# Reordering VectorE's list and the turn of the choice in the experts' stage of a four-layer program

## The reference

```
# layer 0, first half: a routed and shared feed-forward with top 2 of 8 experts per token -> x
# layer 0, second half: "expert choice", added to its input
scores = einsum('BTC,CE->BTE', x, gate_w)
probs  = softmax(scores)                        # over the 8 experts
top_p, top_idx = top_k(transpose(probs), cap)   # each expert takes 8 of the 32 tokens of a sequence
xin = take_along_axis(x, top_idx)
h   = gelu(einsum('BElC,ECH->BElH', xin, w1))   # H = 512
y   = einsum('BElH,EHC->BElC', h, w2) * top_p
out = zeros.at[b, top_idx].add(y)
# layers 1 to 3: an LSTM, an RNN and a leaky cell, each with a feed-forward
```

## Time and profile before

| | us |
|---|---|
| median of 3 runs | 560.34 |
| lowest, highest | 558.55, 560.71 |
| the profiled execution, its own time | 560.55 |
| its span in the profile | 559.2 |
| PE busy | 526.6 (94%) |
| DVE busy | 435.0 (78%) |
| ACT busy | 358.9 (64%) |
| POOL busy | 181.8 (33%) |

### The profile page before, as it was taken

How to read it: one execution, slowest core, us unless ns; L and a number is a source line. 1 busy time by engine, 2 the same in 40 slices (tenths; PEclk the granted TensorE clock), 3 DMA queues, 4 the chain that set the end, 5 groups by cost and what they waited for, 6 DMA issues and landing times.

```text
span 559.2 us, 10400 instructions
## 1 busy us (share of the span) xinstructions
PE 526.6 (94%) x3320; PEld 452.9 (81%) x3320; DVE 435.0 (78%) x1135; ACT 358.9 (64%) x814; POOL 181.8 (33%) x188
## 2 busy tenths in 40 slices
PE   8999999999976998989999989899999999999997
PEld 7877886777766887978989977788999999997785
DVE  4987668467654589797876458998999999999966
ACT  4567753474534556355443346898888888888965
POOL 4688785773000577890730000001100000000100
PEclk9999999999999999989999999999999999999999
DMA  8635943343898422301200000113111111112111
GB/s 283 190 151 222 358 155 103 76 182 81 253 307 242 137 50 57 102 0 39 98 1 1 1 1 0 21 26 33 21 21 19 21 30 29 30 30 56 39 57 39
DMA packets 50405, 49.83 MB, mean 89 GB/s; under 512 B 23264, under 2 KB 42752, under 8 KB 49792
## 3 DMA queue, kind: packets, MB, share of 16 engines
q1 hardware_dynamic: 48304, 44.84, 26.9%
q0 software_dynamic: 2048, 4.33, 2.6%
HBM read 37.87 MB, written 10.69 MB: 87 GB/s over the span
## 4 chain that ended last, share of the span: by engine, by line
PE 63%; DVE 15%; SPq 8%; issue 5%; POOL 3%; DMA 3%; ACT 3%; DVEq 0%; ACTq 0%
PE bank L1718 6%; PE bank L370 5%; PE bank L372 5%; PE bank L371 5%; PE bank L2157 4%; PE bank L2243 4%; PE bank L2147 4%; SPq L888 3%; PE bank L2184 3%; PE bank L2185 3%; POOL y_rows L1025 3%; SPq L856 2%; DMA w_ring<-routed_w 2%; PE bank L1788 2%; DVE scat L1843 2%
## 5 line engine op out<-in xcount | busy, mean ns | idle before, releaser
L2538 POOL CAST h_high<-h 128x256 fp32r<-128x256 f32 x15 | 6.4, 425 | 197.7 <-ACT h L2349 191.3
L1025 POOL DMA_INDIRECT y_rows<-routed_y,slot_at x32 | 32.5, 1017 | 64.0 <-DMA routed_y<-y_out 54.6
L370 PE MATMUL bank<-xin_high,sw_high 128*128 128x256 f32 x128 | 43.8, 343 | 4.0 <-DVE sw_low L1691 3.5
L2184 PE MATMUL bank<-taps_high,q1T 128*128 128x512 f32 x94 | 43.1, 459 | 1.0 <-ACT q1T L2312 0.6
L846 POOL DMA_INDIRECT routed_x<-x_rows,slot_at x32 | 31.9, 996 | 17.2 <-issue 11.5
L2185 PE MATMUL bank<-taps_low,q1T 128*128 128x512 f32 x94 | 37.1, 394 | 0.0
L2147 PE MATMUL bank<-x,lstm_wx 128*128 128x128 f32 x256 | 34.4, 277 | 1.7 <-ACT gates_t L2285 0.9
L371 PE MATMUL bank<-xin_low,sw_high 128*128 128x256 f32 x128 | 36.0, 281 | 0.0
L2285 ACT ACTIVATE gates_t<-bank,lstm_b_half 128x128 f32<-128x128 f32 x96 | 28.3, 365 | 12.1 <-PE bank L2157 8.7
L372 PE MATMUL bank<-xin_high,sw_low 128*128 128x256 f32 x128 | 35.9, 281 | 0.0
L2147 PEld LDWEIGHTS bank<-x,lstm_wx 128*128 128x128 f32 x256 | 32.0, 191 | 4.5 <-ACT gates_t L2285 3.3
(11 more groups left out here) (325 smaller groups left out, 1757.2 us busy)
## 6 DMA issues: line engine op xcount, KB each, us to landing
big<-gates_scratch SPq DMA_DIRECT2D x3, 2048.0 KB, 7.5
w_ring<-routed_w SPq DMA_DIRECT2D x39, 132.0 KB, 3.1
w<-in_f_w SPq DMA_DIRECT2D x16, 256.0 KB, 4.5
onehot<-topi_scratch SPq DMA_DIRECT2D x8, 512.0 KB, 4.8
routed_y<-y_out SPq DMA_DIRECT2D x13, 204.0 KB, 3.6
xs<-routed_x SPq DMA_DIRECT2D x13, 192.0 KB, 3.6
outT<-x SPq DMA_DIRECT2D x15, 128.0 KB, 2.0
xT<-in_xT SPq DMA_DIRECT2D x3, 512.0 KB, 7.4
```

What stands on the lines that cost most here:

```text
L370: pe.matmul(dst, wh[:, cols], vh[:, :], start=start, stop=False)
L1025: pool.indirect_dma_start(y_rows[c % 2][:, r, i, :], None, ys_dram[:, :], bass.IndirectOffsetOnAxis(slot_at[:, r, tile:tile + 1], 0)).then ...
L2184: pe.matmul(dst, q, taps_high[:, 2 - j, :], start=True, stop=False)
```

## The change

Nothing is added or taken away; pieces move in the lists of VectorE and TensorE. In groups 0 and 1:

- `combine` of the two chunks moves from ahead of the copies of experts 4 and 6 to behind the copies of experts 5 and 6; `choice_scores` follows the second one; `choice_probs` moves behind the split and copy of expert 7;
- scatter tables move from rounds 4 to 7 (four each) to rounds 2 (eight), 4 (four) and 7 (four, behind the copy);
- `choice_transpose` moves from the end of the group to unit 2 of the next group, ahead of its down part; `choice_tables` and `choice_rows` move to behind the copy of expert 0 of the next group; TensorE's wait for `probT` moves from unit 0 to unit 4.

```diff
--- before.py
+++ after.py
@@ -1877,8 +1877,11 @@
                     w = g * U2 + u
                     if w + LEAD < GROUPS * U2:
                         expert_up(w + LEAD)
-                    if g in (1, 2) and u == 0:
+                    if g in (1, 2) and u == 4:
                         pe.wait_ge(s_dc, g * TABLES + TURNED)
+                    if g in (1, 2) and u == 2:
+                        pe.wait_ge(s_ye, g * E + 1)
+                        choice_transpose(g, y_bank[0][:, SIDE])
                     expert_down(w)
                     if g and u == 0:
                         slots_turn(g - 1, 1)
@@ -1902,9 +1905,6 @@
                         slots_transpose(1, m_bank[0])
                     if u == (10 if g == GROUPS - 1 else 14):
                         slots_turn(g, 0)
-                    if g < 2 and u == U2 - 1:
-                        pe.wait_ge(s_ye, g * E + E - 1)
-                        choice_transpose(g + 1, y_bank[0][:, SIDE])
                     if g == GROUPS - 1 and u in (13, 14):
                         scatter_early(u - 13)
 
@@ -1941,24 +1941,19 @@
                             expert_split(k + 3)
                         residual(g - 1, 0)
                         residual(g - 1, 1)
-                    if g < 2 and e in (4, 6):
-                        combine(DENSE + 2 * g + e // 2 - 2)
-                    if g < 2 and e == 6:
-                        choice_scores(g + 1)
-                    if g < 2 and e == 7:
-                        choice_probs(g + 1)
                     if g < GROUPS - 1:
                         if e in (1, 3):
                             tokens_low(g + 1, e // 2)
                         if e in ((2, 4) if g == 0 else (3, 4)):
                             gather_onehot(g + 1, (e - 2) // 2 if g == 0 else e - 3)
-                    if g == 2:
+                    if g < 2:
+                        if e in (2, 4):
+                            scatter_tables(g, range(8) if e == 2 else range(8, 12))
+                    elif g == 2:
                         if e == 7:
                             scatter_tables(g, range(8, 16))
-                    else:
-                        tables_at = 2 if g == GROUPS - 1 else 4
-                        if tables_at <= e < tables_at + 4:
-                            scatter_tables(g, range(4 * (e - tables_at), 4 * (e - tables_at + 1)))
+                    elif 2 <= e < 6:
+                        scatter_tables(g, range(4 * (e - 2), 4 * (e - 1)))
                     if k + 3 < GROUPS * E and not (g and e == 1):
                         expert_split(k + 3)
                     output_copy(g, e)
@@ -1968,9 +1963,17 @@
                     if g == 2 and e == 6:
                         slots_copy(1, m_bank[0])
                         scatter_tables(g, range(8))
-                if g < 2:
-                    choice_tables(g + 1, y_bank[0][:, SIDE])
-                    choice_rows(g + 1)
+                    if g < 2:
+                        if e in (5, 6):
+                            combine(DENSE + 2 * g + e - 5)
+                        if e == 6:
+                            choice_scores(g + 1)
+                        if e == 7:
+                            scatter_tables(g, range(12, 16))
+                            choice_probs(g + 1)
+                    if 1 <= g < 3 and e == 0:
+                        choice_tables(g, y_bank[0][:, SIDE])
+                        choice_rows(g)
 
             for eng in (pe, dve):
                 eng.wait_ge(s_down, ALL_UNITS)
```

## The result

The changed kernel takes **565.1 us** (median of 6 runs, 563.4 to 566.9) against 560.45 for the kernel before in the same comparison. The ratio is **1.0075, with a 95% interval of 1.0053 to 1.0097**: slower by 4.2 us, between 3.0 and 5.4. The profiled execution took 565.57 us, 1.27 of them around its span.

The account below looks back on a forecast made before the run. The prediction took TensorE, busy 526.6 of 559.2 us, as the bound. Terms of 0 (group 0), -0.3 (group 1), +3.4 (clock) and +0.5 (group 2) sum to +3.6 on 560.34, giving 564.0 us; range 559.3 to 566.0.

Parts of the forecast that it names:

- The waits that go: TensorE in groups 0 and 1: waits for splits, `probT` and one-hots disappear, up to 6.8 us altogether.
- The list of group 0: VectorE behind unit 11: 8.96 us of work, scores at 216.4, unit 16 at 219.7 against 219.69 before.
- The term of 0: Group 0: three waits of 3.25 us become one of at least 3.25 for a Gelu, same date; 0 us.
- The list of group 1: VectorE behind unit 27: about 10.7 us, combinations 4.1 each, unit 32 at 258.1 against 258.37; term -0.3.
- The clock: TensorE's clock falls behind each of the two Gelu waits, 1.7 us each; term +3.4, bounds 0 and 3.4.
- the stall at 156 to 158: TensorE's DMA stall before the experts' stage: granted clock stayed at 1.00, so a 3 to 4 us stall may not lower it.
- Group 2: GpSimd's later tap work covers the first 1.3 us of VectorE's sixteen scatter tables; term +0.5, bounds 0 and 1.4.
- Clock falls once: Rival: the first Gelu wait is spared a fall of TensorE's clock; 562.3 us, chance 0.22.
- never: Rival: TensorE's clock falls behind neither Gelu wait, the change only renames waits; 560.6 us, chance 0.13.
- Exponentials reached in time: Rival: at the end of groups 0 and 1 ScalarE gets the scores early enough; 552 or 556 us, chance 0.14.
- A rule on the table load: ScalarE before each group: skill adds 1380 ns drain per table switch, each start 1.4 us later; term kept 3.3.
- A rule on the clock: TensorE: skill advises against long idle gaps between matmul bursts, as the clock falls to half; speaks against the change.

Follow-up runs that it names:

- e1: Changed kernel with the choice's exponentials moved on ScalarE behind the Gelu of unit 2 of the next group; 557.99 us, ratio 0.9956 to the kernel before.
- e7: Changed kernel with each group's first combination behind the copy of expert 4 instead of expert 5, exponentials unmoved; 560.1 us, ratio 0.9993 to the kernel before.
- e3: Changed kernel plus unread TensorE products (18 and 22) during the Gelu waits before units 16 and 32; 561.89 us, ratio 1.0023 to the kernel before.
- e5: Changed kernel with the choice's turn, tables and `probT` wait back in their old places, leaving VectorE's new order alone; 564.6 us, ratio 1.0069.
- e2: Kernel before with only the late turn of the choice, VectorE's order in groups 0 and 1 as before; 558.19 us, ratio 0.9944.
- e6: Kernel before with the late turn and the exponentials behind the Gelu of unit 2, combinations in the old order; 565.8 us, ratio 1.0087.
- e9: As e6, with the choice's last step (`choice_probs`) moved behind the split and copy of expert 7; 558.69 us, ratio 0.9963 to the kernel before.
- e8: Changed kernel with late exponentials, first combinations behind expert 4's copy, and group 2's last eight tables behind expert 7's copy; 553.1 us, ratio 0.9872.

## Why the prediction was right, and where it was off

The forecast was 564.0 us and slower; 565.1 was measured, inside the range. The mechanism was the one forecast; that the total came within 1.1 us owes something to luck, where errors met (below). By its own steps:

- **The waits that go.** Right: `sw_low`, `probT` and one-hot waits are all gone. Unit 11 starts at 206.74, which without the shift of 0.37 is the 206.4 that the working used.
- **The list of group 0.** Right to 0.1 us: scores done at 216.61 + 0.23 - 0.37 = 216.5, against 216.4; unit 16 at 220.05 - 0.37 = 219.68 against 219.7. The term of 0 holds, and e1 and e7 show its cause: three waits had become one, behind the scores.
- **The list of group 1.** The mechanism was right, one size off. I took 4.1 us for a combination; they took 3.70 and 3.58, since the clock had made the list later: only one of GpSimd's long pieces began beside the first one, and its work ended at 255.5, beside the second one. e3, without the slow clock, shows 4.52 and 3.82, 8.3 us together, close to the 8.2 that I had used. Estimate and surroundings belonged together. The date of unit 32 came out right by luck: 259.96 without the shift, against 258.1 + 1.7 = 259.8. The clock cost 0.9 us more than I took, and the list was 1.0 us shorter.
- **The clock.** This is the mis-sized term. I took 1.7 us for each fall, from the one in the earlier trace rows, and wrote 3.4. e3 shows 2.6 and 2.9 where they fall, and 4.05 net in the stage. The step that failed was to carry the size of the fall in before over to the two new ones: there the clock was low for 3.4 us, here for 6.8 each time, 5.4 and 6.0 of them in TensorE's work. The length of the wait alone does not give the size: behind 4.73 us in e5 it was 3.4 us again. The other thing wrong was to take for a sign that the stall at 156 to 158 leaves the clock alone. It did so in before and e5; in the other nine profiles the clock fell behind that stall, or near its end.
- **Group 2.** Right: tables 4.59 instead of 4.20, turn wait 1.1 instead of 0.7, +0.4 for a term of +0.5. The cover was not as I laid it out, though. I set the later end of GpSimd's tap work (288.7) against the old start of the tables (287.78), as if they did not move. In after the tap work ended at 293.0, since its load was issued 9.6 us later and not 5, and the tables began at 292.37: a cover of 0.65 us instead of 1.3. That the size came out is luck; in e2, with 1.2 us of cover, the tables took 5.09.
- **The rivals.** "Clock falls once" and "never" fell by the windows of the profiled execution; in two of the other five the mean clock leaves room for less than two full falls. "Exponentials reached in time" fell by ScalarE's waits of 5.7 and 6.3 us; e1 shows what it would have met next, the copy of expert 7. The half of the change that costs is the order on VectorE with the exponentials left where they are; the late turn is a gain by itself (e2), which I had costed only as part of a sum that came to nothing.
- **A rule on the table load.** The row pair 218.11 with 1.28 us and 219.40 leaves 0.01 us between load and Gelu. By the drain that the Trainium skill adds ("ScalarE: Activation LUTs", section "What ACT_TABLE_LOAD costs") unit 16 would have started 1.4 us later, an estimate from that page's figure; the trace does not agree with it here.
- **A rule on the clock.** Gaps of 2.8 to 6.0 us lowered the clock in the stage in after, e1, e5, e6 and e7 (with one exception in e6, below), and with the gaps filled by products that nobody reads (e3) it stayed up. The Trainium skill, "TensorE: Matmul & The Clock Gate" (section "Why this matters for your kernels"), warns of idle gaps between bursts; in the main this case agrees.

Open: the stretch from unit 35 to unit 48 was 0.4 us shorter in after than in before. All of it lies in unit 39, which took 2.44 us in before and 2.02 to 2.05 in all the others; the profile shows 0.17 us of idle time there and names no engine for it.

## What to carry to other kernels

Before putting "urgent" work first on an engine, follow the work that it displaces to its own last reader: here the scores, then ScalarE's exponentials, then the Gelu queued behind them, then TensorE. Several short waits and one wait of their sum end at the same date but are not worth the same; the long one is more likely to lower TensorE's clock, and that is paid in busy time afterwards (5.4 us in e3's comparison). If an order is right only once another engine's piece is off the path, move both ends of that handover together (e6 and e9 differ by one piece and 7 us).

## What was unexpected of the hardware

- A fall of the clock cost 2.6 us behind a wait of 4.0 and 2.9 behind one of 4.6, against 1.7 read from before. The clock was low for 6.8 us each time, against 3.4 in before. What counts is the part of it behind the wait: in e5, behind waits of 4.7 and 6.0, that was only 2.8 and 3.0 us; in e1, behind a wait of 3.4, it was 5.9.
- The length of one wait does not settle whether the clock falls. Waits of up to 2.0 us did not lower it in e2 and e9, one of 2.2 with a shorter one close by did in before, and both of 2.78 did in e7's profile. But of e6's two turn waits of 3.18 and 3.12 us only the first did. The stall on a transfer at 156 to 158 us shows the same without any difference in the kernel there: it lasted 3.07 and 3.19 us in before and e5 and the clock stayed up, and it fell in the other nine profiles, behind stalls of 2.38 (e8) to 4.20 us (after). What sets these apart stays open, and one execution's row can't settle it.
- A slow clock on TensorE can shorten VectorE's work elsewhere, by timing: it moved the combinations of group 1 against GpSimd's pieces, and the two took 7.3 us in after against 8.3 in e3. In these rows VectorE loses at the beginning of each long GpSimd piece, not for its whole length.
